# Six tiles for the group-norm statistics, loaded ahead of the weights; first outputs scaled ahead of the input's low parts; last four biases between the next image's snapshots

## The reference, cut to what matters

```
h = group_norm(hidden_states, norm_gamma, norm_beta)
q, k, v = conv1x1(h, wq, bq), conv1x1(h, wk, bk), conv1x1(h, wv, bv)
attn = softmax(einsum('bci,bcj->bij', q, k) * 512 ** -0.5, axis=2)
out = conv1x1(einsum('bcj,bij->bci', v, attn), wo, bo)
return residual + out
```

## Time and profile before

| | |
|---|---|
| median of 3 runs | 2090.39 us (2090.16 to 2092.7) |
| the profiled execution: its own time | 2089.34 us |
| its span (first to last instruction) | 2087.7 us |
| PE, DVE, ACT, POOL busy | 97%, 78%, 46%, 16% |
| mean granted TensorE clock | 0.988 of full speed |
| matmuls | 8848, of which 16 x 540 in the images |

### The profile page before, as it was taken

How to read it: one execution, slowest core, us unless ns; L and a number is a source line. 1 busy time by engine, 2 the same in 40 slices (tenths; PEclk the granted TensorE clock), 3 DMA queues, 4 the chain that set the end, 5 groups by cost and what they waited for, 6 DMA issues and landing times.

```text
span 2087.7 us, 27170 instructions
## 1 busy us (share of the span) xinstructions
PE 2019.2 (97%) x8848; PEld 1663.5 (80%) x8848; DVE 1623.4 (78%) x2112; ACT 957.1 (46%) x1427; POOL 327.4 (16%) x236
## 2 busy tenths in 40 slices
PE   7699999999999999999999999999999999999998
PEld 6478788888888888788788888888888888878887
DVE  2769697786968869697786968869697886968856
ACT  2635463453645435463453645435363452645442
POOL 1002012020211202012020211202012120211202
PEclk8699999999999999999999999999999999999999
DMA  3433434252353233434243353333434243253302
GB/s 121 185 128 118 135 151 111 81 140 102 149 140 151 44 137 120 131 151 111 88 133 111 140 141 151 49 132 125 126 151 119 99 113 134 117 141 151 73 29 41
DMA packets 57124, 248.79 MB, mean 119 GB/s; under 512 B 8208, under 2 KB 8208, under 8 KB 50192
## 3 DMA queue, kind: packets, MB, share of 16 engines
q1 hardware_dynamic: 36032, 214.97, 26.8%
q0 software_dynamic: 18432, 33.56, 10.9%
q10 hardware_dynamic: 2640, 0.01, 0.1%
HBM read 208.15 MB, written 73.92 MB: 135 GB/s over the span
## 4 chain that ended last, share of the span: by engine, by line
PE 61%; DVE 16%; DMA 13%; issue 6%; ACT 3%; SPq 1%; DVEq 0%; POOL 0%; ACTq 0%; POOLq 0%
PE bank L304 20%; PE bank L306 20%; PE bank L305 20%; DMA room<-in_x 13%; DVE h_lo L725 5%; DVE wide L927 3%; DVE scores L933 2%; DVE bn L660 2%; DVE scores L919 2%; ACT scores L595 1%; DVE scores L921 1%; DVE big_lo L906 1%; DVE scores L886 0%; ACT big_hi L590 0%; ACT scores L563 0%
## 5 line engine op out<-in xcount | busy, mean ns | idle before, releaser
L304 PE MATMUL bank<-big_hi 128*128 128x512 f32 x1056 | 411.9, 390 | 0.8 <-DVE big_lo L733 0.8
L306 PE MATMUL bank<-big_hi,big_lo 128*128 128x512 f32 x1056 | 411.5, 390 | 0.0
L305 PE MATMUL bank<-big_lo,big_hi 128*128 128x512 f32 x1056 | 411.5, 390 | 0.0
L304 PE MATMUL bank<-big_hi,h_hi 128*128 128x512 f32 x896 | 350.5, 391 | 16.0 <-ACT room L622 16.0
L306 PE MATMUL bank<-big_hi,h_lo 128*128 128x512 f32 x896 | 349.4, 390 | 0.0
L305 PE MATMUL bank<-big_lo,h_hi 128*128 128x512 f32 x896 | 349.1, 390 | 0.0
L622 ACT COPY room<-bank 128x512 f32<-128x512 f32 x192 | 113.0, 589 | 318.4 <-PE bank L306 190.0
L304 PEld LDWEIGHTS bank<-big_hi 128*128 128x128 f32 x1056 | 198.8, 188 | 42.3 <-DVE big_lo L733 1.2
L305 PEld LDWEIGHTS bank<-big_lo,big_hi 128*128 128x128 f32 x1056 | 198.8, 188 | 41.6
L660 DVE BATCH_NORM_STATS2 bn<-room 128x6 f32<-128x512 f32 x128 | 86.7, 692 | 186.7 <-DMA room<-in_x 186.2
L306 PEld LDWEIGHTS bank<-big_hi,big_lo 128*128 128x128 f32 x1056 | 198.6, 188 | 41.1
(11 more groups left out here) (102 smaller groups left out, 3385.4 us busy)
## 6 DMA issues: line engine op xcount, KB each, us to landing
w_split<-kept_t SPq DMA_DIRECT2D x15, 3584.0 KB, 11.2
w_split<-kept_v SPq DMA_DIRECT2D x16, 3072.0 KB, 10.5
out<-scores POOLq DMA_DIRECT2D x128, 256.0 KB, 6.7
room<-in_x SPq DMA_DIRECT2D x120, 256.0 KB, 2.9
room<-in_x SPq DMA_DIRECT2D x30, 1024.0 KB, 6.0
kept_t<-w_split SPq DMA_DIRECT2D x1, 3584.0 KB, 10.6
room<-in_x SPq DMA_DIRECT2D x4, 512.0 KB, 10.2
kept_v<-big_hi SPq DMA_DIRECT2D x1, 1536.0 KB, 5.1
```

The lines of the kernel that those rows point to most:

```text
L304: nc.tensor.matmul(o, a_hi, b_hi, start=start, stop=False, skip_group_check=True)
L305: nc.tensor.matmul(o, a_hi, b_lo, start=False, stop=False, skip_group_check=True)
L306: return nc.tensor.matmul(o, a_lo, b_hi, start=False, stop=stop, skip_group_check=True)
```

## The change

**SP.** Before, SP waited until the T products of the image were done, issued the load of `kept_v`, and then the eight pieces into two tiles of `room` by turns, each piece after the one two before it had been read. Now there are six tiles for the pieces: two of `room`, two of `red`, two of `wide` (`red` and `wide` serve the softmax at other times). The first two pieces are issued when the low parts of the image are done (`h_split`), four more when all outputs of the image before are scaled (`o_scaled`), all ahead of `kept_v`; the last two come behind `kept_v`, into tiles 0 and 1, when pieces 0 and 1 have been read.

**DVE.** The statistics are taken six and two at a time, in the place of four and four. Outputs 0 to 3 are scaled ahead of six `low_h`, in the place of behind them.

**ACT.** Outputs 4 to 7 get their bias in the next image's turn: 4 and 5 behind snapshot a, 6 and 7 behind snapshot b. Before, all eight stood ahead of snapshot a. The last image has all eight at its end, as before.

```diff
+        pieces = [a[:, n, :] for a, n in ((room, 6), (room, 7), (red, 0), (red, 1), (wide, 0), (wide, 1))]
...
-        piece_in = [sem("piece_in0"), sem("piece_in1")]
+        piece_in = [sem(f"piece_in{n}") for n in range(6)]
...
+                def piece(n):
+                    k, half = divmod(n, 2)
+                    sp.dma_start(pieces[n % 6],
+                                 x_d[b + 1][:, k, half * HALF:(half + 1) * HALF]).then_inc(piece_in[n % 6], 16)
+                if more:
+                    sp.wait_ge(h_split, count(b, 7, 7))
+                    for n in range(2):
+                        piece(n)
+                    sp.wait_ge(o_scaled, count(b, 8, 8))
+                    for n in range(2, 6):
+                        piece(n)
                 sp.wait_ge(t_summed, count(b, 14, 14))
                 sp.dma_start(w_split[:, :, 0:VW].bitcast(F32), kept_v).then_inc(wvs_in, 16)
                 if more:
-                    for n in range(PIECES):
-                        if n < 2:
-                            sp.wait_ge(h_split, count(b, 7, 7))
-                        else:
-                            sp.wait_ge(bn_set, count(b, PIECES, PIECES + n - 1))
-                        k, half = divmod(n, 2)
-                        sp.dma_start(room[:, 6 + n % 2, :],
-                                     x_d[b + 1][:, k, half * HALF:(half + 1) * HALF]).then_inc(piece_in[n % 2], 16)
+                    for n in range(6, PIECES):
+                        sp.wait_ge(bn_set, count(b, PIECES, PIECES + n - 5))
+                        piece(n)
...
             def image(b, more, first=False):
                 act.wait_ge(h_split, count(b, 7, 7))
                 for r in range(2):
                     if r == 0:
                         snap(b, r, 0, "a", T_AT[4])
+                        if not first:
+                            for n in (KC, KC + 1):
+                                bias_output(b, n, last=True)
                     snap(b, r, 1, "b", T_AT[2])
+                    if r == 0 and not first:
+                        for n in (KC + 2, KC + 3):
+                            bias_output(b, n, last=True)
...
-                for n in range(2 * KC):
+                for n in range(KC):
                     bias_output(b, n)
+                if not more:
+                    for n in range(KC, 2 * KC):
+                        bias_output(b, n)
...
                     if more and pair == 0:
-                        for n in range(4):
+                        for n in range(6):
                             next_piece(b, n)
...
                     if more and pair == 0:
-                        for n in range(4, 8):
+                        for n in range(6, 8):
                             next_piece(b, n)
...
                 inverse(b, 0)
+                dve.wait_ge(sum_step, count(b, SUM_STEPS, SUM_STEPS))
+                for n in range(KC):
+                    output(b, n)
                 if more:
                     for n in range(1, 7):
                         low_h(b + 1, n)
                     dve.wait_ge(h_split, count(b + 1, 7, 7))
-                for n in range(KC):
-                    output(b, n)
                 inverse(b, 1)
                 for n in range(KC, 2 * KC):
                     output(b, n)
```

More of the change, by code:

```diff
@@ L590, in high_p, with bias_output, image @@
                 nc.scalar.copy(p_hi[:, j, :], scores[:, half * NJ + j, :]).then_inc(p_high, 1)
-            def bias_output(b, n):
+            def bias_output(b, n, last=False):
                 c = n % KC
-                act.wait_ge(o_scaled, count(b, 8, 8 + n + 1))
+                act.wait_ge(o_scaled, count(b, 8, (0 if last else 8) + n + 1))
                 nc.scalar.activation(scaled(n), scaled(n), ACT.Identity,
                                      bias=out_bias[:, c:c + 1]).then_inc(o_done, 1)
-            def image(b, more):
+            def image(b, more, first=False):
                 act.wait_ge(h_split, count(b, 7, 7))
@@ L651, in image @@
                     high_h(b + 1, 6)
-                for n in range(2 * KC):
+                for n in range(KC):
                     bias_output(b, n)
-            images(act, image)
+                if not more:
+                    for n in range(KC, 2 * KC):
+                        bias_output(b, n)
+            image(0, True, True)
+            with act.Fori(1, B - 1) as b:
+                image(b, True)
+            image(B - 1, False)
         @block.vector
@@ L662, in next_piece @@
             def next_piece(b, n):
-                dve.wait_ge(piece_in[n % 2], count(b, 64, 16 * (n // 2 + 1)))
-                bn_piece(n, room[:, 6 + n % 2, :])
+                if n < 2 or n >= 6:
+                    dve.wait_ge(piece_in[n % 6], count(b, 32, 16 * (n // 6 + 1)))
+                else:
+                    dve.wait_ge(piece_in[n], count(b, 16, 16))
+                bn_piece(n, pieces[n % 6])
             def channel_stats(b):
```

## The result

The changed kernel takes 2060.47 us (median of 4 runs, 2057.07 to 2062.84), the kernel before 2090.89 in the same comparison: ratio 0.9852, 95% interval 0.9835 to 0.9869. That is 1.5% faster where 1.9% was forecast (2051), inside the range. The profiled execution took 2057.07 us.

What follows compares the result with a forecast made beforehand. PE's matmuls were taken to bound the kernel, with two stalls an image beside them. Removing both, 20.2 + 19.0 = 39.2 us, takes 2089.34 to 2050.1, as a median 2051.2 us, 1.9% faster; range 2048 to 2063.

Steps and rivals of the forecast that it cites:

- What bounds: PE's matmuls: 540 of 0.2267 us, 122.4 us an image; only two stalls, in T and S, come on top.
- the sum: Whole kernel: 20.2 + 19.0 = 39.2 us off the profiled 2089.34, giving 2050.1; as a median 2051.2.
- Part 1: Early pieces end PE's stall in S for the copies into `room`: 15 images x 1.35 = 20.2 us.
- Part 2: Later biases end PE's stall in T for ACT's snapshot a: 15 boundaries x 1.27 = 19.0 us.
- Part 3: DVE's first outputs sooner: low parts cost nothing; without it D3's high part comes after 839.8 and pushes snapshot y.
- What is late next: Stores 4 to 7, which `add_t` D3 of r = 1 awaits before S; new PE wait between 0 and 0.8 us.
- I take 0: PE's new wait at S's start taken as none, since 844.4 and 847.9 are both ahead of 848.1.
- The case that had 0.77: The forecast itself: both stalls gone, new waits under 0.2 us an image, 2051.2 us; chance 0.77.
- rival A: Stores late at `add_t` D3 of r = 1, up to 0.8 x 15 = 12 us, 2051 to 2063; chance 0.13.
- the sign that was named for it: A wait of PE for DVE's low parts at the start of S.
- The landing: Store 7's data arrival: 844.4 by the stores' stream alone, 847.9 at worst with 3.5 us of pieces fully added.
- D3's latest start: `add_t` D3 of r = 1 on DVE may start at 848.1 at the latest, for S's first low part at 851.9.

Runs made afterwards that it cites:

- e1_pieces_later: Changed kernel with pieces 2 to 5 issued only when nine products of T are done; 2050.2 us, 0.9830 of the kernel before.
- r2: Changed kernel with pieces 2 to 5 issued after nine products of T, run again on another chip; 2049.0 us, 0.9796 of the kernel before.
- u1_pieces_only: Kernel before with only the six piece tiles loaded ahead of the weights, biases and DVE's order as before; 2069.5 us, ratio 0.9898.
- u3_old_biases: Changed kernel with all eight biases ahead of snapshot a again; 2073.9 us, 0.9921 of the kernel before.
- u4_old_dve_order: Changed kernel with outputs 0 to 3 scaled behind the low parts again; 2060.2 us, 0.9855 of the kernel before.
- u5_later_old_order: Changed kernel with pieces 2 to 5 after nine products of T and outputs 0 to 3 behind the low parts; 2051.9 us, ratio 0.9813.
- r1: The changed kernel itself run once more, on one chip with r2; 2061.1 us, 0.9847 of the kernel before.
- e3: Changed kernel with output 4's bias ahead of snapshot a and 5, 6, 7 between snapshots a and b; 2050.7 us, 0.9837 of the kernel before.
- e4: Changed kernel with pieces 2 to 5 after nine products of T, one bias ahead of snapshot a, three behind; 2049.5 us, ratio 0.9831.
- e2: Changed kernel with all six early pieces, not four, issued beside the stores; 2073.0 us, 0.9940 of the kernel before.
- u2_no_pieces: Changed biases and DVE order, but the pieces in two tiles behind the weights as before; 2068.2 us, 0.9903 of the kernel before.

## Why the prediction was right, and where it was off

- **What bounds.** Right: 0.2267 us a matmul, 122.40 us an image, and nothing else. The kernel with the sharing taken away has just that in each of 14 images (e1_pieces_later). That its profiled execution took 2050.22 us where the sum said 2050.1 is in part luck: it ran on a chip on which the kernel before takes 2084.9, so its gain there was 34.7 us, and 42.9 on the chip of r2, where the sum has 39.2.
- **Part 1, 20.2 us.** Right in the total, by u1_pieces_only (2069.5, forecast 2070) and by the six statistics in a row. The 1.35 an image was a little too much, since the mean of the earlier trace rows has the first image's 2.5 us in it: the other images lose 1.23. The first image, with its clock at 0.50 behind the stall, won more than it was charged.
- **Part 2, 19.0 us.** The stall was 1.27 us, as u1_pieces_only leaves it; ACT fitted at all three snapshots, none of which PE waits for.
- **Part 3, "cost nothing", and needed against "push snapshot y".** The low parts cost nothing. But part 3 puts DVE's outputs 4 to 7 about 0.3 us later (u3_old_biases), and its gain was over-sized: 0.1 us an image (u4_old_dve_order, u5_later_old_order), not the more than 1 that was expected there. The wait for stores 0 to 3 was rightly found under the name of a snapshot.
- **What is late next.** This is the step that was off: "I take 0". The case that had 0.77, new waits under 0.2 us an image, did not come. What came was rival A, with 0.13: 0.70 us an image (123.10 - 122.40) between its bounds 0 and 0.8, with its place and its mechanism, and with the sign that was named for it: the first product of S (837.22) comes 0.2 us late, right behind DVE's low parts (834.00 + 3.09 = 837.09). The total stayed in the range because the range had A in it.
- **The terms behind that 0.** The landing was put between 844.4 and 847.9 where PE's start of T was 832.82, so 11.6 to 15.1 us into T, and D3's latest start at 848.1, 15.3 us into T. In the 14 images with pieces the last store landed 15.4 us into T in the mean, and D3 started at 15.7. Both terms of the 15.1 were off. The stream of the stores alone takes until 12.9 (e1_pieces_later), 1.3 us more than the 11.6; the pieces add 2.5, not 3.5. So that the worst case comes within 0.3 us of what happened is in part two errors against each other. In the pair r1, r2 the pieces add 2.8 us (15.6 and 12.8), with the sooner biases 3.2 (14.6 in e3, 11.4 in e4), and two more pieces add 1.1 (16.5 in e2). The rule of the Trainium skill (DMA: Bandwidth & Descriptors, Queues, rings and completion order), that the engines serve their queues by turns whoever issued, gave 847.9, that is 15.1 us into T. The traces agree that stores and pieces delay each other: with the pieces beside them the last store landed 2.5 us later. No run shows whose packets were served when.
- **Where PE waits first.** The first product to wait was not the one that was named: product 1 of r = 1 needs the D3 sum at 16.3 us into T, before S needs its low part.
- **The total.** 0.70 us in 15 images is 10 us, and 2051 + 10 = 2061 against 2060.5 measured. That it closes to 0.5 us is in part luck too: an image had 2.50 us to win and not 2.62, and the first image gave 5.7 where it was charged 1.35.

## What to carry to other kernels

A transfer moved out of one queue's way lands in another's: before moving loads ahead, list the stores that are in flight then and what waits for the last of them, and charge the traffic to it, not none (2.5 to 3.2 of 3.5 us here). Where the worst case of a sum leaves 0.2 us of slack, one term that is 1.3 us short is enough for a wait, so don't take the wait at 0. A load that isn't wanted until late can be held back behind the stores: one wait more ahead of it was worth 12 us here (r1, r2).

## What the runs showed of the hardware

Four loads of 256 KB beside four accumulating stores of 256 KB delayed the last store by 2.5 us in the mean (landing at 15.4 us into T, and at 12.9 with the loads held back), where the loads' own traffic is 3.5 us, an estimate at the rate of `kept_v`. Over 820.8 to 833.1 the engines were 0.85 busy at 171 GB/s; the weights' load right after, 3 MB in 10.3 us, ran at about 300 in the mean. The window row of the changed kernel at this place:

```profile
820.80:833.10 12.30, 12.30 (x56) 10.20 (x55) 5.56 (x9) 7.38 (x13) 3.46 (x4) 1.00 0.85 171
```

After each of these stalls the next step of PE is slower: 0.34 us in the place of 0.23 for the step from 834.14 to 834.48 above, though the granted clock stays at 1.00. A stall of 0.2 us therefore cost half as much again. After the 2.5 us stall of the first image of the kernel before, the granted clock was 0.50 for 3.4 us; behind the first image's stall of 1.2 us in u2_no_pieces it stayed at 1.00.
